# Deflation in a batched eigensolver: two of four scan rows as columns instead of rows repeated on all partitions

## The reference, cut to what matters

```python
deg = jnp.sum(A, axis=-1)
d_isqrt = jax.lax.rsqrt(deg)
Lap = deg[..., :, None] * jnp.eye(n, dtype=A.dtype) - A
Lap_norm = d_isqrt[..., :, None] * Lap * d_isqrt[..., None, :]
_, U = jnp.linalg.eigh(Lap_norm)
agg = jnp.einsum('bmn,bmd->bnd', U, features)
h = jax.nn.relu(jnp.einsum('bnd,hd->bnh', agg, W0) + b0)
out = jnp.einsum('bnh,oh->bno', h, W1) + b1
ret = jnp.einsum('bnm,bmo->bno', U, out)
```

## Time and profile before

| what | before |
| --- | --- |
| time, median of 3 runs | 6235.88 us (6235.08 to 6240.02) |
| time of the profiled execution | 6238.06 us |
| its span | 6235.6 us |
| VectorE busy | 4778.0 us (77%) |
| TensorE busy | 2528.0 us (41%) |
| ScalarE busy | 1724.1 us (28%) |
| DMA moved | 140.48 MB, mean 23 GB/s |

### The profile page before, as it was taken

The page is one execution under the profiler, slowest core; times in us unless marked ns, Lnnn a source line. Parts: engine busy times, 40 slices in busy tenths (PEclk is TensorE's granted clock), DMA queues, the critical chain, the costliest instruction groups (busy, mean ns, idle before and its releaser), DMA issues.

```text
span 6235.6 us, 61923 instructions
## 1 busy us (share of the span) xinstructions
PE 2528.0 (41%) x16242; PEld 1636.1 (26%) x16242; DVE 4778.0 (77%) x19142; ACT 1724.1 (28%) x6552; POOL 81.4 (1%) x45
## 2 busy tenths in 40 slices
PE   1545444444329173471918115601069400100089
PEld 0212112222215141331506114501057400100066
DVE  4666666666689999999985797598978599899812
ACT  0000000000132323313214112327534344324245
POOL 0000000000000000000000000000010000000000
PEclk9666666655558577685859557855589755555599
DMA  5000000000000000000010200310000200200021
GB/s 121 12 14 27 15 15 16 17 19 21 24 16 14 7 14 7 7 7 8 0 14 14 49 0 7 76 27 0 0 7 15 103 0 0 94 0 0 0 68 41
DMA packets 142053, 140.48 MB, mean 23 GB/s; under 512 B 28445, under 2 KB 128426, under 8 KB 134826
## 3 DMA queue, kind: packets, MB, share of 16 engines
q1 hardware_dynamic: 141738, 136.97, 8.0%
HBM read 110.43 MB, written 26.41 MB: 22 GB/s over the span
## 4 chain that ended last, share of the span: by engine, by line
DVE 56%; PE 29%; DMA 6%; ACT 4%; issue 3%; SPq 1%; DVEq 0%; POOL 0%; ACTq 0%; PEldq 0%; POOLq 0%
PE psum L1898 7%; DVE big_b L1043 4%; PE psum L1556 3%; DVE gvec L362 2%; DMA big_b<-rows_dram 2%; ACT big_a L2008 2%; PE psum L1918 2%; PE psum L1611 1%; PE psum L1617 1%; DVE big_a L1053 1%; DVE big_a L1051 1%; PE psum L1615 1%; DVE big_b L1041 1%; DVE big_b L1047 1%; DVE big_b L1046 1%
## 5 line engine op out<-in xcount | busy, mean ns | idle before, releaser
L1898 PE MATMUL psum<-big_a 128*32 128x508 f32 (+59 forms) x4032 | 445.7, 613 | 39.4 <-ACT big_a L1861 39.4
L2066 PE MATMUL psum<-big_b 128*128 128x128 f32 x384 | 71.7, 372 | 844.7 <-ACT big_b L1984 844.7
L2076 PE MATMUL psum<-plane,big_b 128*128 128x128 f32 x192 | 36.0, 366 | 816.7 <-DVEq L1186 800.3
L1505 PE MATMUL psum<-plane,big_a 128*128 128x128 f32 x192 | 49.9, 428 | 650.6 <-ACT big_a L1421 628.6
L2008 ACT ACTIVATE big_a<-big_a 128x128 f32<-128x128 f32 (+1 forms) x896 | 241.8, 271 | 238.8 <-DVE big_a L1053 163.6
L2066 PEld LDWEIGHTS psum<-big_b 128*128 128x128 f32 x384 | 69.4, 284 | 847.0 <-ACT big_b L1984 847.0
L1864 ACT COPY big_a<-psum 128x64 f32<-128x64 f32 x126 | 33.4, 265 | 895.2 <-PE psum L1904 895.2
L2076 PEld LDWEIGHTS psum<-plane,big_b 128*128 128x128 f32 x192 | 32.0, 192 | 818.9 <-issue 800.9
L1556 PE MATMUL psum<-big_b 128*128 128x512 f32 x544 | 244.3, 611 | 0.0
L1043 DVE RECIPROCAL big_b<-big_b 128x512 f32<-128x512 f32 x70 | 234.7, 3353 | 2.4
L355 DVE TENSOR_TENSOR dot_parts<-psum,plane 128x8 f32<-128x8 f32 (+6 forms) x109 | 20.8, 191 | 274.7 <-PE psum L1898 274.7
(11 more groups left out here) (695 smaller groups left out, 10027.9 us busy)
## 6 DMA issues: line engine op xcount, KB each, us to landing
big_a<-rows_dram SPq DMA_DIRECT2D x4, 4096.0 KB, 12.2
vt<-pairs_dram SPq DMA_DIRECT2D x504, 32.0 KB
big_a<-rows_dram SPq DMA_DIRECT2D x4, 2048.0 KB, 17.2
big_a<-rows_dram SPq DMA_DIRECT2D x2, 3072.0 KB, 19.1
big_b<-rows_dram SPq DMA_DIRECT2D x2, 3072.0 KB, 25.9
big_b<-adj SPq DMA_DIRECT2D x2, 2048.0 KB, 17.5
big_b<-adjT SPq DMA_DIRECT2D x2, 2048.0 KB, 39.2
lap_dram<-big_b SPq DMA_DIRECT2D x4, 1024.0 KB, 11.2
```

The source lines that it names most:

```text
L1505: ins = t.transpose(psum[0:parts, bank, g * N:(g + 1) * N], src(g), ident)
L1898: ins = t.matmul(psum[i * SPAN:i * SPAN + MW, 0, 0:4 * wide], v_masked[:, i, q * MW:(q + 1) * MW], anode[:, g:g + 4, k + 1:N + 2 * u], sta ...
L2066: ins = t.matmul(bank(4, g), deflate[:, g, :], w_full[:, g, :], start=True, stop=True)
L2076: ins = t.transpose(bank(0, g), sec[:, g, :], ident)
```

## The change

Of the four scan kinds, `w_new` and `e_new` are used only in a product with a plane that has at most one 1 per partition and graph. After the change they come as columns: `NODE_COLS` gets two more entries, the second one read one element earlier, so that partition p holds the value of node p - 1 (the plane `super` is zero on a block's first partition). The rows of these two kinds are still computed and stored, but no longer loaded: the loads take every second of the four kinds, into slots 0 and 2. In `deflation` the two products read the repeated columns, and the first of them stands in front of the wait. `cols` grows from 8 to 9 columns of 64.

```diff
--- before.py
+++ after.py
@@ -188,7 +188,7 @@
         vt = sb("vt", [N, B, N])
         left, right = vt[:, 0:16, :], vt[:, 16:32, :]
         v_a, v_b, v_u, v_s = (vt[:, 32 + 8 * n:40 + 8 * n, :].rearrange("p a b -> p (a b)") for n in range(4))
-        cols = sb("cols", [N, 8, B])
+        cols = sb("cols", [N, 9, B])
         g_d = sb("g_d", [B, N])
         g_z = sb("g_z", [B, N])
         g_ds = sb("g_ds", [B, N])
@@ -716,7 +716,7 @@
         sc_w = big_a[0:B, 0:17 * N].rearrange("g (i n) -> g i n", n=N)
         scan_h = big_a[:, 17 * N:17 * N + 12 * 64].rearrange("p (i n) -> p i n", n=64)
         ms = sb("ms", [N, 30, B])
-        col_names = ("rank", "pole", "weight", "on", "d", "zn", "dn")
+        col_names = ("rank", "pole", "weight", "on", "d", "new", "e_new", "zn", "dn")
         col = {n: cols[:, i, :] for i, n in enumerate(col_names)}
 
         def v_level_rows(v, st, lp, lev):
@@ -967,7 +967,8 @@
 
         NODE_COLS = (("rank", lambda: g_rank[:, :]), ("pole", lambda: g_rows[:, ROWS.index("pole"), :]),
                      ("weight", lambda: g_rows[:, ROWS.index("weight"), :]), ("on", lambda: g_onout[:, :]),
-                     ("d", lambda: g_dall[:, :]))
+                     ("d", lambda: g_dall[:, :]), ("new", lambda: g_rows[:, ROWS.index("w_new"), :]),
+                     ("e_new", lambda: g_rows[:, :, :].rearrange("g r n -> g (r n)")[:, ROWS.index("e_new") * N - 1:ROWS.index("e_new") * N + N - 1]))
 
         def v_level_merge(v, st, lp, lev):
 
@@ -981,7 +982,7 @@
                 st(v.tensor_copy(cols[:, i, :], psum[:, 2, i * B:(i + 1) * B]))
             v.sem_inc(S("to_node_read"), 1)
             cmp_ = lambda ap: ap.rearrange("p (g n) -> p g n", n=blk)
-            keep_r, new_r, ekeep_r, enew_r = (cmp_(row_tiles[:, i, :]) for i in range(4))
+            keep_r, ekeep_r = cmp_(row_tiles[:, 0, :]), cmp_(row_tiles[:, 2, :])
             diff, wx, z_r = (tuple(cmp_((row_tiles[:, 4 + i, :], second_tiles[:, i, :])[h]) for h in both) for i in range(3))
             mt, mr = cmp_(m_t), cmp_(m_r)
             allg = lambda ap: over(ap, gs_, 1)
@@ -1000,11 +1001,11 @@
 
                 def deflation(h):
 
+                    lp(v.tensor_tensor(mt, perp(cb("new"), h), allg(diag_c), ALU.mult))
                     v.wait_ge(S("scan_rows_in"), i * (16 * nb * halves) + (loaded + 16 * nb * h))
-                    lp(v.tensor_tensor(mt, new_r, allg(diag_c), ALU.mult))
                     lp(v.tensor_tensor_scan(m_r, row_tiles[:, 0, :], m_t, 0.0, ALU.mult, ALU.add))
                     lp(v.tensor_tensor(mr, mr, ekeep_r, ALU.mult))
-                    lp(v.tensor_tensor(mt, enew_r, allg(super_c), ALU.mult))
+                    lp(v.tensor_tensor(mt, perp(cb("e_new"), h), allg(super_c), ALU.mult))
                     lp(v.tensor_tensor(keep_r, mr, mt, ALU.add))
                     v.sem_inc(S("deflate_ready"), 1)
 
@@ -2234,12 +2235,12 @@
 
                     sy.wait_ge(S("deflate_spread"), i * PAIR[lev] + (SOLVES[lev] + 1))
                     sy.wait_ge(S("solved"), i + (PAIRED[lev] + 1))
-                    rows_from(row_tiles[:, 0:4], slice(0, 4), 0, "scan_rows_in")
+                    rows_from(row_tiles[:, 0:4:2], slice(0, 4, 2), 0, "scan_rows_in")
                     rows_from(row_tiles[:, 4:7], slice(4, 7), 0, "pole_rows_in")
                     if PAIR[lev] == 2:
                         rows_from(second_tiles, slice(4, 7), 1, "pole_rows_in")
                         sy.wait_ge(S("deflate_spread"), i * PAIR[lev] + (SOLVES[lev] + 2))
-                        rows_from(row_tiles[:, 0:4], slice(0, 4), 1, "scan_rows_in")
+                        rows_from(row_tiles[:, 0:4:2], slice(0, 4, 2), 1, "scan_rows_in")
             sy.wait_ge(S("turn_stored"), 16 * GROUPS)
             sy.wait_ge(S("eig_done"), 1)
             od = outs["out"].rearrange("g n c -> n g c")
```

## The result

The changed kernel takes 6204.42 us (median of 5 runs, 6202.28 to 6206.99) against 6235.88 us for the kernel before (5 runs, 6232.36 to 6241.77): a ratio of 0.9948, 95% interval 0.9933 to 0.9963, 31.5 us less. The forecast was 6206.7 us. Its profiled execution has a span of 6201.5 us.

A forecast was written before the change was run, and what follows sets the result against it. Load phases were taken to end with the last bytes landing in one queue. Transfers -29.7 us plus register work 0.5 gave -29.2: profiled 6238.06 to 6208.9, less 2.2 to the median, forecast 6206.7 us, range 6201 to 6219.

The forecast's parts named there:

- The place: Level 32, level 64 and both pairs of level 128: VectorE's two waits for scan and pole rows, together 93.9 us.
- What a row costs: Price per row kind: 4.98 us at level 32, 4.85 at 64, 2.50 at 128; dropping two kinds gains 29.7 us.
- The cover of deflation: First halves: deflation ends before the last landing, so VectorE still idles 3.5 us or more in front of L1013.
- Rival (a): Level 32 alone: shorter or split transfers run slower per byte, up to 9.96 us, 6216.7 at worst; chance 0.07.
- Rival (b): Products in the three second halves: the repeated column costs two passes, 12.8 us given back, 6219.5; chance 0.02.
- (d): Deflation's products with the repeated column first run element by element, four times as long (9.2 us), time 6258; chance 0.02.
- Register work: Level 128's second halves: column addresses come from a register, two new instructions in each, 4 x 0.13 = 0.5 us.
- Rival (c): Second pair of level 128: something of ScalarE's is late, 4 us given back, time 6211; chance 0.03.

## Why the prediction was right

**The place.** The wait rows named four load phases, and what was reckoned came out in them: 29.3 us in the mean against 29.7. Forecast from issue to copy 27.5, 43.2, 21.8 and 22.3 us, measured over three profiles 26.9, 42.4 to 42.7, 22.1 to 23.8, 22.1 to 22.2. The pages count 140.48 MB before and 125.81 after, the 14.7 MB less that were forecast.

**What a row costs.** Per kind 4.98, 4.85 and 2.50 us: in sum 14.8 us for one kind in all phases. Measured 144.7, 130.9, 114.7 us for four, three and two kinds, so 13.8 and 16.2, 15.0 in the mean. The sum of 29.7 us came out as 29.3, in part by luck. In the means the places gave 10.3, 10.4, 3.6 and 5.0 us where 9.96, 9.70, 5.01 and 5.01 were reckoned: the first two gave 1.1 us more together, the third 1.4 less.

**The cover of deflation.** Reckoned 3.5 us at its smallest; measured 3.43 to 3.48 us in the changed kernel. The kernel with the product behind the wait shows that this cover is real, and the one with four kinds that nothing else of the change shortens a load phase.

**Rival (a), shorter transfers.** Level 32's transfers fell to 512 KB in pieces of 8 KB, and the phase ended 0.6 us before the forecast, not after it. The estimate from the Trainium skill, "DMA: Bandwidth & Descriptors", sections "Bandwidth" and "Anatomy of one DMA" (1.45 times the cost per byte, 4.5 us less gained), did not come true here, where the transfers stand behind one another in one queue. The Trainium skill gives those figures for transfers that GpSimd issues; here SyncE does.

**Rival (b) and (d), the column.** L1004 and L1008 with the column first take 2293 and 2292 ns at the median, as L1173 said.

**Register work.** 57 to 71 ns in front of L1008; in a second half of level 128 the two products come 0.11 and 0.12 us later than before, 0.46 us in all, forecast 0.5.

**Rival (c), ScalarE.** In the second pair its preparation ended at 5403.79 + 2.00 and the spread began at 5405.70, 1.6 us after deflation's end at 5404.07, as reckoned (1.7). Nothing that ends the pair waited for it: from the copy to TensorE's first group at the end the pair took 469.2 us, before 469.1.

**What was off.** The first pair of level 128 gave 3.0 us instead of 5.0 in the first profile. Of the five profiles with one queue, the undivided wait and fewer than four kinds (the changed kernel three times, three kinds, product behind the wait) four show 1.3 to 1.7 us more in this phase than in the second pair; with four kinds it is not there, nor in the two kernels with a second queue and an undivided wait, whose loads at level 128 are the same as the changed kernel's (22.27 and 21.75 us). The DMA issues on the page of the changed kernel's first profile and of its second (over both pairs of level 128: KB each, median us to landing) tell where the time goes:

```profile
big_a<-rows_dram SPq DMA_DIRECT2D x2, 3072.0 KB, 15.0
...
big_b<-rows_dram SPq DMA_DIRECT2D x2, 3072.0 KB, 21.9
```

```profile
big_a<-rows_dram SPq DMA_DIRECT2D x2, 3072.0 KB, 14.2
...
big_b<-rows_dram SPq DMA_DIRECT2D x2, 3072.0 KB, 21.1
```

Taken by pair, the first half's pole rows (`big_a`) landed after 15.9 us in the first pair and 14.1 in the second of the first profile, the second half's (`big_b`) after 22.7 and 21.0. The scan rows were in use 7.4 and 7.1 us after their issue. So the delay is there before the last transfer ends: it arises with the first half's pole rows. Why stays open; it costs about 1 us in the mean.

**What the sum does not hold.** The time fell by 31.5 us, and by 30.0 and 33.4 in the two later comparisons, against a forecast of 29.2. The 4.9 us behind the last load phase are no part of what was reckoned. In 13 profiles this stretch took 490.8 to 497.5 us with the same instructions in it. Its length varies between executions of one kernel, as shown; but both profiles of the kernel before are at the long end, and the other eleven have a mean of 492.3 us. The times say something alike: in the eleven comparisons with a changed kernel the time fell by 4.3 us more, in the mean, than that kernel's load phases (-0.3 to 9.4; 4.3 us with all four kinds loaded). Nearly all of these lie within their noise, and they share four sets of runs of the kernel before; together they lean towards some 4 us that the columns bring and the prediction does not have. That is not shown, and what would bring it was not looked for.

## What to carry to other kernels

Ask of a load what waits for its last byte: bytes are worth their time only there, and here the price per row could be read between two waits on the same queue. After such a cut, look at what the wait covers that is not needed yet: a semaphore of its own for the rows used later was worth 21 us more of load phase, and 17.8 us of time beside the changed kernel, with no byte less. Moving the product in front of the wait was worth nothing, because another landing ended later.

## What the runs showed of the hardware

A load into 64 partitions ran at 210 GB/s and one into 128 at 434 GB/s in the windows shown, in 8 KB pieces in both cases. Loads into 32 partitions at a time cost 4.98 us per 1024 KB, which is 210 GB/s in the mean; in windows of 4 us at level 32 of the two first profiles the rate went from 131 to 264 GB/s. The Trainium skill, "SBUF — State Buffer", section "Door 1: The DMA port swizzle", gives partitions 0 to 63 one half of the 16 ports and the other 64 the other half, which fits these two rates. Two queues for the two halves gave 244 and 246 GB/s in the windows shown, not 430, and why stays open.

TensorE's granted clock at the end of a level was 0.58 of full speed (near the lower of its levels, 1.2 of 2.4 GHz) in one execution and 1.00 in another, behind the same 288 us of idleness and the same work, and two profiles of one and the same kernel show 1.00 and 0.56 there; such stretches, and the 519 to 526 us between levels 32 and 64, spread by 5 to 7 us between profiles and bound what a change of 0.1% can be told from.
